# A batched graph layer on one core: the joined result is turned by VectorE in 32x32 blocks, and added on GpSimd

## What is computed

```
h   = max(layernorm(x), 0)                      # [512, 128]
HW  = h @ W[r, :128] + c[r]                     # r = 0..6, c[r] = W_edges[r] @ W[r, 128:]
A   = [adj, adj, I, adj^T, adj^T, I, I]         # per batch
out = x + bias + max over r of (A[r] @ HW[r])   # [512, 128]
```

## Time and profile before

| | |
|---|---|
| median of 3 runs | 233.76 us (233.65 to 235.31) |
| the profiled execution: its time, its span | 235.21 us, 233.3 us |
| PE busy | 221.1 us, 95% of the span |
| ACT, DVE, POOL busy | 186.1, 178.2, 143.3 us |
| DMA packets | 30385, 34.52 MB |

### The profile page before, as it was taken

How to read it: one execution, slowest core, us unless ns; L and a number is a source line. 1 busy time by engine, 2 the same in 40 slices (tenths; PEclk the granted TensorE clock), 3 DMA queues, 4 the chain that set the end, 5 groups by cost and what they waited for, 6 DMA issues and landing times.

```text
span 233.3 us, 4799 instructions
## 1 busy us (share of the span) xinstructions
PE 221.1 (95%) x1133; PEld 182.5 (78%) x1133; DVE 178.2 (76%) x387; ACT 186.1 (80%) x468; POOL 143.3 (61%) x163
## 2 busy tenths in 40 slices
PE   7898787999999999999999999999999999999983
PEld 5777565788888888888888888888888888888762
DVE  4796578578687978778687978778787978768564
ACT  3868788578898988888898988888898988886650
POOL 2580786629668484939669494949669493946300
PEclk9999999799999999999999999999999999999999
DMA  5926215933726445263726435373736436303203
GB/s 189 325 69 225 93 42 186 255 121 114 231 97 199 161 125 181 102 222 121 233 96 206 154 121 182 104 230 111 220 112 203 157 109 205 93 7 116 105 3 90
DMA packets 30385, 34.52 MB, mean 148 GB/s; under 512 B 2103, under 2 KB 20135, under 8 KB 30375
## 3 DMA queue, kind: packets, MB, share of 16 engines
q1 hardware_dynamic: 30375, 34.41, 45.3%
HBM read 30.14 MB, written 4.26 MB: 147 GB/s over the span
## 4 chain that ended last, share of the span: by engine, by line
PE 82%; DVE 6%; DMA 3%; issue 3%; POOL 2%; ACT 1%; SPq 0%; DVEq 0%; ACTq 0%
PE rel_ps L718 10%; PE at_ps L686 10%; PE rel_ps L720 10%; PE rel_ps L719 10%; PE fwd_ps L718 6%; PE fwd_ps L720 6%; PE fwd_ps L719 6%; PE bwd_ps L718 6%; PE bwd_ps L720 6%; PE bwd_ps L719 5%; PE turn_ps L714 3%; PE turn_ps L698 3%; DMA a_sb<-in_adj 2%; DMA x_sb<-in_x 1%; POOL a_lo L265 1%
## 5 line engine op out<-in xcount | busy, mean ns | idle before, releaser
L265 POOL TENSOR_TENSOR a_lo<-a_sb,a_hi 128x512 fp32r<-128x512 f32 x62 | 79.0, 1294 | 55.7 <-ACT a_hi L333 55.7
L540 DVE TENSOR_TENSOR best<-rel_ps,best 128x512 f32<-128x512 f32 x62 | 42.4, 684 | 17.4 <-PE rel_ps L720 16.7
L381 ACT ACTIVATE rel_ps<-sum_all,c_col 128x512 f32<-128x512 f32 (+1 forms) x63 | 41.8, 679 | 6.7 <-DVE best L540 4.3
L511 DVE TENSOR_TENSOR at_lo<-at_ps,at_hi 128x512 fp32r<-128x512 f32 x62 | 41.1, 683 | 6.7 <-ACT at_hi L341 6.7
L333 ACT ACTIVATE a_hi<-a_sb 128x512 fp32r<-128x512 f32 x64 | 39.4, 617 | 3.7 <-DMA a_sb<-in_adj 3.7
L341 ACT ACTIVATE at_hi<-at_ps 128x512 fp32r<-128x512 f32 x62 | 36.3, 590 | 7.2 <-PE at_ps L686 7.2
L686 PE MATMUL at_ps<-ident,a_sb 128*128 128x128 f32 x240 | 31.5, 273 | 0.0
L686 PEld LDWEIGHTS at_ps<-ident,a_sb 128*128 128x128 f32 x240 | 28.0, 141 | 4.3 <-DVE at_lo L511 0.2
L537 DVE SCALAR_TENSOR_TENSOR best<-rel_ps,c_col,best 128x512 f32<-128x512 f32 x32 | 24.0, 750 | 7.4 <-PE rel_ps L720 6.2
L718 PE MATMUL fwd_ps<-at_hi,h_hi 128*128 128x512 f32 x64 | 27.1, 424 | 1.2 <-issue 0.7
L718 PE MATMUL bwd_ps<-a_hi,h_hi 128*128 128x512 f32 x64 | 26.9, 420 | 0.0
(11 more groups left out here) (104 smaller groups left out, 443.0 us busy)
## 6 DMA issues: line engine op xcount, KB each, us to landing
a_sb<-in_adj SPq DMA_DIRECT2D x64, 256.0 KB, 4.1
sum_all<-sums_dram SPq DMA_DIRECT2D x16, 512.0 KB, 3.6
x_sb<-in_x SPq DMA_DIRECT2D x16, 256.0 KB, 2.9
out<-o_sb SPq DMA_DIRECT2D x15, 256.0 KB, 2.3
w_sb<-in_L_gnn_W SPq DMA_DIRECT2D x1, 448.0 KB, 5.9
bias_sb<-in_L_gnn_b SPq DMA_DIRECT2D x1, 256.0 KB, 5.0
sums_dram<-sum_rows SPq DMA_DIRECT2D x16, 4.0 KB
out<-o_sb SPq DMA_DIRECT2D x2, 128.0 KB, 1.9
```

Of the source, the lines that this page charges most:

```text
L265: pool.tensor_tensor(a_lo[q][:, j, :], a_sb[q][:, j, :], a_hi[q][:, j, :].bitcast(fp32), ALU.subtract).then_inc(a_lo_ready[j], 1)
L381: act.activation(to[:, cols], sum_all[q][:, 0 if r in FWD else 1, cols], ACT.Copy, scale=c_col[:, r:r + 1]).then_inc(after_it, 1)
L511: dve.tensor_tensor(at_lo[q][:, i, :], at_bank(b, i)[:], at_hi[q][:, i, :].bitcast(fp32), ALU.subtract).then_inc(at_lo_ready[i], 1)
L540: dve.tensor_tensor(best[q][:], held[:], best[q][:], ALU.max).then_inc(joined[r], 1)
```

## The change

PE no longer turns `best`. DVE transposes it from SBUF to SBUF in blocks of 32x32 at the end of its step (`turn_best`), so that `turned` holds, in partition 32g + n and column 32c + f, node 32c + n and feature 32g + f. x and the bias are loaded once more in that layout (`xp_sb`, `bias_sb`), and `add_bias` reads `xp_sb`. The final addition moves to POOL (`finish`, ahead of `add_bias` in the step). The store, too, goes by blocks. Each of these transfers is four, one for each 32 features, with runs of 32 floats (128 bytes) in DRAM. SP's step is reordered, and so is the start: `spread_sums` of batch 0 is first, POOL makes xb of batches 0 and 1 in its first step. `reload_x` no longer waits for xb. The end does the last batch in two halves on DVE, transpose and addition, with no PE.

```diff
+            def load_by_blocks(to, nodes, loaded):
+                for g in range(G):
+                    sp.dma_start(to[g * Q:(g + 1) * Q, :].rearrange("n (c f) -> n c f", f=Q),
+                                 by_blocks(nodes)[g]).then_inc(loaded, 16)
+            def store_by_blocks(nodes, held, cols, stored):
+                for g in range(G):
+                    sp.dma_start(by_blocks(nodes)[g],
+                                 held[g * Q:(g + 1) * Q, cols].rearrange("n (c f) -> n c f", f=Q)).then_inc(stored, 16)
             def reload_x(k, q):
-                b = 2 * k + q
-                sp.wait_ge(h_ready, b + 1)
-                sp.wait_ge(xb_ready, b + 1)
+                sp.wait_ge(h_ready, 2 * k + q + 1)
                 load_x(k + 1, q)
+            def reload_xp(k, q):
+                sp.wait_ge(xb_ready, 2 * k + q + 1)
+                load_by_blocks(xp_sb[q], x[2 * k + 2 + q, :, :], xp_loaded[q])
             def step(k, q, more, stored=True):
-                if stored:
-                    store(k - 1, q)
+                if isinstance(k, int) and k == 0 and q == 0:
+                    spread_sums(k, q)
                 if more:
                     reload_x(k, q)
                     reload_a(k, q)
-                spread_sums(k, q)
+                    reload_xp(k, q)
+                if stored:
+                    store(k - 1, q)
+                if not (isinstance(k, int) and k == 0 and q == 0):
+                    spread_sums(k, q)
...
-            sp.dma_start(bias_sb[:], bias.rearrange("(j p) o -> p j o", p=P)).then_inc(bias_loaded, 16)
+            load_by_blocks(bias_sb, bias, bias_loaded)
+            for q in range(2):
+                load_by_blocks(xp_sb[q], x[q, :, :], xp_loaded[q])
...
+            def finish(k, q):                                  # on POOL
+                b = 2 * k + q
+                pool.wait_ge(best_turned, b + 1)
+                pool.wait_ge(xb_ready, b + 1)
+                wait(pool, out_stored[q], G * 16 * k)
+                pool.tensor_tensor(o_sb[q][:], turned[q][:], xb_sb[q][:], ALU.add).then_inc(out_ready, 1)
...
                     if left:
                         reciprocal_std(*after(k, q))
+                    finish(k - 1, q)
                     add_bias(k, q)
...
+            def turn_best(k, q):                               # on DVE, last in a step
+                b = 2 * k + q
+                dve.wait_ge(joined[ORDER[-1]], b + 1)
+                wait(dve, out_ready, b - 1)
+                dve.transpose(turned[q][:], best[q][:]).then_inc(best_turned, 1)
...
-                    finish(k - 1, q)                           # DVE, first in a step
...
-                    turn_best(*prev, b + 2)                    # PE, last in a step
...
             dve.wait_ge(xb_ready, B)
-            dve.wait_ge(out_stored[1], 16 * (PAIRS - 1))
+            dve.wait_ge(out_stored[1], G * 16 * (PAIRS - 1))
...
+                dve.wait_ge(joined_, count)
+                dve.transpose(turned[q][:, cols], best[q][:, cols]).then_inc(half_turned, 1)
+                dve.wait_ge(half_turned, half + 1)
+                dve.tensor_tensor(o_sb[q][:, cols], turned[q][:, cols], xb_sb[q][:, cols],
+                                  ALU.add).then_inc(half_out_ready, 1)
```

More of the change, by code:

```diff
@@ L34, in gnn_layer @@
     S = 2 * C
+    Q = 32
+    G = P // Q
     PAIRS = B // 2
@@ L70, in gnn_layer @@
         x_sb = pair(sb, "x_sb", [P, C, F])
-        xb_sb = pair(sb, "xb_sb", [P, C, F])
+        xp_sb = pair(sb, "xp_sb", [P, N])
+        xb_sb = pair(sb, "xb_sb", [P, N])
         h_sb = pair(sb, "h_sb", [P, C, F])
@@ L92, in gnn_layer @@
         best = pair(sb, "best", [P, N])
-        o_sb = pair(sb, "o_sb", [P, C, O])
+        turned = pair(sb, "turned", [P, N])
+        o_sb = pair(sb, "o_sb", [P, N])
         at_ps = pair(bank, "at_ps")
@@ L240, in _ @@
             store(PAIRS - 1, 0)
[L241 to L246, removed]
+            for half in range(2):
+                sp.wait_ge(half_out_ready, half + 1)
+                cols = slice(half * HALF, (half + 1) * HALF)
+                store_by_blocks(out[B - 1, cols, :], o_sb[1], cols, out_stored[1])
+            sp.wait_ge(out_stored[0], G * 16 * PAIRS)
+            sp.wait_ge(out_stored[1], G * 16 * (PAIRS + 1))
         @block.gpsimd
@@ L289, in first_step @@
                                    ALU.subtract).then_inc(w_lo_ready, 1)
-                pool.wait_ge(bias_loaded, 16)
+                pool.wait_ge(bias_loaded, G * 16)
                 add_bias(0, 0)
+                add_bias(*ahead)
             def step(k, q, left):
@@ L299, in step @@
                     split_a(k, q, 3)
-                    add_bias(k, q)
                 else:
@@ L324, in _ @@
             later_batches(pool, step)
+            finish(PAIRS - 1, 0)
         @block.scalar
@@ L664, in _ @@
             dve.wait_ge(xb_ready, B)
-            dve.wait_ge(out_stored[1], 16 * (PAIRS - 1))
-            for half, (turned, count, after_it) in enumerate(((half_turned, 1, half_out_ready),
-                                                              (best_turned, B, out_ready))):
+            dve.wait_ge(out_stored[1], G * 16 * (PAIRS - 1))
+            for half, (joined_, count) in enumerate(((half_joined, 1), (joined[BWD[1]], B))):
                 cols = slice(half * HALF, (half + 1) * HALF)
-                dve.wait_ge(turned, count)
-                dve.tensor_tensor(o_sb[1][:].rearrange("p j o -> p (j o)")[:, cols], at_ps[half][:, cols],
-                                  xb_sb[1][:].rearrange("p j o -> p (j o)")[:, cols], ALU.add).then_inc(after_it, 1)
+                dve.wait_ge(joined_, count)
[3 more added lines that the diff above has]
+                                  ALU.add).then_inc(half_out_ready, 1)
         @block.tensor
@@ L691, in turn_h @@
                 pe.wait_ge(h_ready, b + 1)
-                if isinstance(b, int) and b == 1:
-                    pe.wait_ge(ht_lo_ready, 1)
-                else:
-                    wait(pe, out_ready, b - 2)
-                    wait(pe, ht_lo_ready, b)
+                wait(pe, ht_lo_ready, b)
                 for j in range(C):
@@ L707, in turn_sums @@
                 pe.transpose(to[0:S, 0:P], sums[q][:].rearrange("p t c -> p (t c)"), ident[:]).then_inc(sums_turned, 1)
-            def turn_best(k, q, ht_count):
-                b = 2 * k + q
-                pe.wait_ge(joined[ORDER[-1]], b + 1)
-                pe.wait_ge(ht_lo_ready, ht_count)
-                for j in range(C):
-                    last = pe.transpose(turn_ps[:, j * P:(j + 1) * P], best[q][:, j * P:(j + 1) * P], ident[:])
-                last.then_inc(best_turned, 1)
             def passes(out, w_hi_, w_lo_, m_hi, m_lo, start, stop, onto=False):
@@ L870, in _ @@
                        False, True, onto=True).then_inc(done, 1)
-            pe.wait_ge(at_lo_ready[3], B)
-            pe.wait_ge(sum_rows_ready, B)
-            for half, (ready, count, after_it) in enumerate(((half_joined, 1, half_turned),
-                                                             (joined[r], B, best_turned))):
-                pe.wait_ge(ready, count)
-                for j in range(half * C // 2, (half + 1) * C // 2):
-                    last = pe.transpose(at_ps[half][:, j * P:(j + 1) * P], best[q][:, j * P:(j + 1) * P], ident[:])
-                last.then_inc(after_it, 1)
 _INS = ["x", "adj", "L0_gnn_W", "L0_gnn_W_edges", "L0_gnn_b"]
```

21 lines of the change are left out of this document (8 added, 13 removed).

## The result

| | before | after |
|---|---|---|
| median | 233.70 us (4 runs) | 249.31 us (4 runs, 247.16 to 251.23) |
| profiled execution: time, span | 235.21, 233.3 us | 247.16, 245.4 us |
| PE, DVE, ACT, POOL busy, share of the span | 95, 76, 80, 61% | 89, 73, 76, 66% |

The ratio is 1.062, with an interval of 1.053 to 1.071; between the medians it is 15.6 us slower. The ratio is one of means, without the execution of 251.23 us, which counts as a slow one (over 1.5% above the fastest). The forecast was 241.5 us in a range of 229.5 to 251: 7.8 us slower, half of what was measured.

The account below looks back on a forecast made before the run. PE's own work bound the steps at 13.14 us. Twelve periods at 13.6 + 0.25 (+8.5), one at 12.92 (-0.2), start -2.6 and end +2.1 gave +7.8, so 241.5 us; range 229.5 to 251, the forecast's own 237 to 246.

Parts of the forecast that it names:

- rival 3: DMA engines: 128-byte packets cost as much as 512-byte ones, or more; period 15.15 us, 257 us in all; chance 0.14.
- PE's four transposes: PE, each step: removing the transposes of `best` saves 0.44 us, leaving 12.70 us as PE's own period.
- `fwd_lo` next: DVE, behind PE: the next pass waits for `fwd_lo`, so the period is at least 12.92 us.
- The transposes on DVE at 0.69: DVE, behind `fwd_lo`: the added transpose takes 0.69 us, fits into waiting time and costs nothing.
- SP, sums later by 3.6 us against a slack of 2.2: SP: eight transfers ahead of `spread_sums` delay the sums 3.6 us; slack is 2.2 us, so ACT's `fill` stalls.
- rival 1: The sums stay in time and DVE's `fwd_lo` sets the period, 12.92 us; 230.4 us in all; chance 0.17.
- The loop of two steps: From `fill` through ACT, POOL, SP, DRAM and back: 27.2 us for two steps, 13.6 us a step.
- q: Queue in front of the sums: time by which it is longer than before, about 0.5 us, 0.25 us per step.
- The start: First steps: load of x freed of its wait for xb and a shorter cast save 2.6 us, ends 0 and 4.5.
- The end: Last batch: the store is eight issues on SP instead of two, 2.1 us more, ends 1 and 3.
- Rival 2: Sums in time and `fwd_lo` early enough, so PE alone sets 12.70 us; 227 us in all; chance 0.05.
- Rival 4: The loop through SP binds only just, 26.6 us, with a better start; everything cancels, 232 to 236 us; chance 0.14.

Follow-up runs that it names:

- ten small issues: Kernel before, with ten transfers of 512 bytes added on SP right ahead of `spread_sums` in every step of the loop: 233.55 us, ratio 0.999.
- fourteen: Kernel before, with fourteen transfers of 512 bytes added on SP right ahead of `spread_sums` in every step of the loop: 248.00 us, ratio 1.062.
- long runs: Changed kernel in its own order, with xp, bias and output in four transfers each with runs of 512 bytes instead of 128: 244.30 us, ratio 1.043.
- the three kernels with its start: Kernels that start as the one before, but for one load of 512 bytes: `join_first` of batch 2 at 42.04 to 42.24 us instead of 43.55.
- the start by itself: Kernel before, with own copy of x for `add_bias`, `reload_x` freed of xb, early xb on POOL, sums of batch 0 first: 229.87 us, ratio 0.983.
- four small ones: Kernel before, with four transfers of 512 bytes added on SP right ahead of `spread_sums` in every step of the loop: 233.70 us, ratio 1.001.

## Why the prediction was right, and where it was off

The sign and the cause were those forecast, but the size was not: 15.6 us slower instead of 7.8. The median, 249.31, lies outside the forecast's own 237 to 246. It is within the full range of 229.5 to 251 only because that range took in the lower part of rival 3, dear packets, which is not what happened; that part is luck. What the prediction named as signs was exceeded too: steps of 13.6 to 14.1 us were forecast and 14.30 measured, waits of 0.5 to 1.5 us for `sum_all` and 1.6 to 2.84 in every second step. The terms that were too small are the loop's start in the first two steps, and what a stall brings with it: a low clock at times, for which the sum had no term.

The span was forecast at 241.1 and came out at 245.4: 13 steps 5.0 us longer than forecast, the start 1.0 better, the end 0.2 worse. The rest to the median, 3.6 us, has two parts. The profiled execution before was 1.5 us over its median, which I had taken off, while that of the changed kernel was 2.1 us under its own: the other three were 1.8 to 4.1 us longer, at mean granted clocks of 0.969 to 0.976 against its 0.986.

**PE's four transposes, 0.44 us a step.** Right: 13.14 - 12.72 = 0.42, shown by putting them back.

**`fwd_lo` next, 12.92.** Right within 0.06: 12.98 with the sums first, 12.72 with `fwd_lo` moved.

**The transposes on DVE at 0.69, with no cost.** Right in both. They are grouped here by line, mean ns of one behind the busy time; the two half ones at the end took 434 ns each.

```profile
L586 DVE STREAM_TRANSPOSE turned<-best 128x512 f32<-128x512 f32 x15 | 10.5, 700 | 0.0
```

**SP, sums later by 3.6 us against a slack of 2.2.** The centre of the forecast, and right. With ten small issues the slack was seen to end at 2.2, with fourteen `fill` was late. An issue took 0.49 for my 0.50. That no row shows one under 0.47 was a slip: the two at the end take 0.45 each. It changes nothing, since rival 1 needed 0.33.

**The loop of two steps, 27.2 us and q.** Right, with one thing missing. The late `fill`s for FWD[0] are at 57.83, 86.31, 116.32, 144.05, 172.09 and 199.59: cycles of 28.5, 30.0, 27.7, 28.0 and 27.5 us. The forecast, 27.2 and 0.5 for q, was 27.7. Two cycles can be followed part by part, from 86.31 and from 116.32. ACT at their ends, then POOL:

```profile
86.31 1.30 ACT L420 ACTIVATE rel_ps<-sum_all,c_col 128x512 f32<-128x512 f32 x2 [2.81 <-DMA sum_all<-sums_dram]
...
116.32 1.30 ACT L420 ACTIVATE rel_ps<-sum_all,c_col 128x512 f32<-128x512 f32 x2 [2.77 <-DMA sum_all<-sums_dram]
```

```profile
95.56 2.55 POOL L295 TENSOR_TENSOR a_lo<-a_sb,a_hi 128x512 fp32r<-128x512 f32 x2 [4.40 <-ACT a_hi L372]
...
102.48 2.72 POOL L295 TENSOR_TENSOR a_lo<-a_sb,a_hi 128x512 fp32r<-128x512 f32 x2
...
123.96 2.55 POOL L295 TENSOR_TENSOR a_lo<-a_sb,a_hi 128x512 fp32r<-128x512 f32 x2 [2.79 <-ACT a_hi L372]
...
130.89 2.72 POOL L295 TENSOR_TENSOR a_lo<-a_sb,a_hi 128x512 fp32r<-128x512 f32 x2
```

and SP in the second (in the first, the rows shown above):

```profile
138.63 0.41 SPq L225 DMA_DIRECT2D sums_dram<-sum_rows  x1
140.21 0.35 SPq L227 DMA_DIRECT2D sum_all<-sums_dram  x1
```

| part | forecast | from 86.31 | from 116.32 |
|---|---|---|---|
| `fill` to POOL's first `a_lo` | 7.65 | 9.25 | 7.64 |
| POOL | 9.26 | 9.64 | 9.65 |
| SP, to the issue of `sums_dram` | 4.65 | 5.01 | 5.02 |
| the 4 KB store and back | 2.08 | 1.62 | 1.58 |
| issue of `sum_all` to `fill` | 3.6 and 0.5 | 4.49 | 3.84 |
| together | 27.7 | 30.0 | 27.7 |

Small misses of the terms cancel in the second. In the first, the first part is 1.6 us longer and the last 0.65. Windows of the changed kernel over the wait and the work behind it, for the first cycle and the second:

```profile
83.00:87.00 4.00, 1.86 (x8) 1.15 (x7) 1.10 (x2) 1.19 (x3) 3.86 (x4) 1.00 0.95 272
87.00:91.50 4.50, 4.45 (x16) 3.68 (x17) 1.81 (x3) 3.07 (x7) 2.16 (x2) 0.63 0.80 202
...
113.00:117.00 4.00, 1.91 (x9) 1.21 (x7) 1.16 (x2) 1.23 (x3) 3.86 (x4) 1.00 0.96 280
117.00:121.50 4.50, 4.44 (x26) 3.86 (x27) 2.62 (x6) 4.10 (x11) 2.23 (x2) 1.00 0.74 192
```

PE had been busy for 1.86 us of 4, with a wait in it, and then worked for 4.5 us at a granted clock of 0.63, a mixture of the levels of 1.2 and 2.4 GHz: 16 instructions, where two steps later the same stretch, behind the same wait, holds 26 at 1.00. ACT's roundings and POOL come later by as much. I counted the wait and not this. It happened behind one of the late `fill`s of this trace, and also once in the kernel with fourteen small transfers (0.62 in 59.4 to 63.9 us) and once in the one with long runs (0.62 in 56.0 to 60.5).

So of the 5.0 us by which the 13 steps are over the forecast, 2.3 are the cycle with the low clock (30.0 against 27.7), of which 1.6 stand behind the low clock and 0.65 are a longer landing, and 0.9 the other four (111.7 against 110.8). Ahead of 57.83 it took 2.9 us more than forecast (17.85 us from the first mark; 14.24 before, and 0.71 for the longer step): the sums came late in the first two steps both (`fill` 2.4 and 3.5 us behind `join_first`, where it stands 0.6 behind it in time), while I had the loop begin with the steps. Behind 199.59 it took 1.1 less.

**q, 0.5 us.** The landing took 0.24 to 0.9 us more and the round trip of the store 0.5 less, so the queue in front of the sums cost less than I had put on it. SP's waits for the store, up to 4.2 us before, were at most 1.9. Packets of 128 bytes took 12.6 ns where I had taken the middle, 17, of 7 and 27. With 12.6 the sum of the prediction is 256 x 0.0126 + 0.9 = 4.1 us, under the 4.65 of issuing, so that the packets by themselves give no q at all; what made the landing longer is open. The Trainium skill (DMA: Bandwidth & Descriptors, Specifications) asks for at least 512 B for line rate. Bytes per time do fall with short runs (128 bytes in 12.6 ns against 512 in 25), but in this kernel that was worth 5 us at most.

**The start, -2.6.** It was -3.6 against the profiled execution before, and -2.1 to -2.3 against the three kernels with its start; both lie within my ends. In the changed kernel the load that had waited for xb is no longer waited for (the row at 33.35), and the cast takes 0.99. But the load of x before it now goes out behind the sums, 4.5 us later than before (21.44 for 16.95), and has a wait of 0.61 that was not there:

```profile
26.39 0.88 DVE L531 BATCH_NORM_STATS2 stats<-x_sb 128x6 f32<-128x128 f32 x4 [0.61 <-DMA x_sb<-in_x]
...
31.25 0.99 DVE L544 CAST h_hi<-h_sb 128x512 fp32r<-128x512 f32 x1 [0.42 <-ACT h_sb L390]
...
33.35 0.87 DVE L531 BATCH_NORM_STATS2 stats<-x_sb 128x6 f32<-128x128 f32 x4
```

In 38 to 45 us of the changed kernel PE is busy for only 5.63 us, since the sums are late there already. With the start by itself, where they are not, it is -4.5, or -3.0 to -3.2 against the three. I put the low clock of the earlier trace rows down to the stall at the start; with the same stall it was absent three times out of four, so the part of my far end that rested on it is not shown.

**The end, +2.1.** It was +2.3.

**The rivals.** Rival 1 (the sums in time, 230.4 us) is the kernel with the sums first: 230.12. Its mechanism was sized rightly (13 steps 2.6 us shorter for 2.9) and was kept from happening by the order on SP alone. Rival 2 (227 us) is the one with `fwd_lo` early, 225.25, better by the start. Rival 3 is out: the share of the DMA engines in a step was 0.66 and 0.64, not near 1, and the long runs took 244 us still. Rival 4 (a loop of 26.6 us) is out: the shortest cycle was 27.5.

**Left open.** What made the clock fall behind one wait and not behind five others, one of them with PE busy for less (1.77 of 4 us in 54.8 to 58.8, then 1.00), no run tells. That the other executions of the changed kernel, up to 4 us longer than the profiled one, had more such stretches fits their lower mean clocks; they have no trace to show it.

## What to carry to other kernels

An engine that issues transfers in order is itself a resource: at about half a microsecond an issue, splitting one transfer in four costs 1.5 us to whatever stands behind it. Put the transfer with a return trip (store, wait, load) first, and the ones with a whole step of room behind it; here that was the difference between 6% slower and 1.6% faster, with the same work. When work leaves the engine that binds, look up what is next, and next again (here the sums, then `fwd_lo`, then PE itself): each was worth a change of order alone. And where a loop through several engines is close to the period, add up its terms over as many steps as it spans: here that gave its length within 3%, in all cycles but the one with the low clock.

## What the runs showed that I had not expected

- A transfer's issue costs SP about the same whatever it moves: ten of 512 bytes 0.45 us each (4.50 / 10), four of 64 KB in 128-byte runs 0.49 (1.97 / 4).
- The 4 KB store was back after 1.3 us with ten or fourteen small transfers between it and the adjacency (1.9 in one step), 2.1 behind the adjacency alone, and mostly 1.6 with the eight of the changed kernel. With four small ones it took longer, 2.2 to 3.0, so that small transfers ahead of it are not what makes it short.
- Equal waits of PE were not followed by equal clocks: 0.63 over 4.5 us behind one, 1.00 behind the next (windows above). Nor were equal starts: 0.76 in 38 to 45 us of the kernel before, 1.00 in three kernels with its start.
